# A graph network's node pass: two products of each block written in rows, their biases added on GpSimd and VectorE

## The chip, the cores and the metric

One core of a Trainium2 chip runs the program. Times are microseconds (us) of one execution on the device. The engines are named as in the profile: PE is TensorE's matmuls, PEld its weight loads, DVE VectorE, ACT ScalarE, POOL GpSimd, SP SyncE, which only issues transfers here.

## The reference, cut to what matters

Four graph layers stand one behind the other on 50,000 nodes of 128 values, 25,000 edges, each in the form `x = x + layer(relu(layernorm(x)))`. All is fp32. What a node gets with no edge, cut to its form:

```python
def own(x):                        # a node without edges
    h = relu(layernorm(x))
    for l in range(5):             # GAT: both heads' mean is h @ mean(W[l]) + bias[l]
        h = h @ W[l].mean(heads) + eb[l].mean(heads) + b[l]
        if l < 4: h = relu(h)
    x = x + h
    h = relu(layernorm(x))         # HGT: gate * ba + (1 - gate) * h
    x = x + gate * ba + (1 - gate) * h
    h = relu(layernorm(x))         # GCN
    x = x + gelu(h @ gcn_W + gcn_b)
    h = relu(layernorm(x))         # typed attention
    return x + h @ cat_W[0] + cat_b
```

The edges' part follows behind, and overwrites the rows of nodes that have some.

## The kernel before, in words

`node_pass` (L319) does the above for all nodes. The nodes are padded to 50,688 and cut into N = 132 blocks of 384 (T = 3 tiles of 128 rows, W = 384). The loop index k of every engine runs over blocks in a software pipeline written out by hand: in its iteration k, an engine does a certain step of block k, another of block k-1, and so on to k-7. Beside the blocks run 98 steps of "slots" (k < 98), two tiles each of gathered rows `xg`, which get their layer norm and scores only. Every engine's instructions go out in the order in which the code lists them; semaphores (one counter an event) tie the engines together.

What each engine does in iteration k, in order:

- **TensorE** (L581): the first product of the GAT chain for block k-1 (L603, features in partitions, 384 nodes moving, into `psZ`); its scores (L605, into `psA`); transposes of the chain's end `zT` of block k-2 back into rows (L613, into `psX`, by the helper `turn`, L584); the slots' scores (L619). Then for r = 1 to 4: product r of the chain (L627, again into `psZ`) and `to_rows` (L592), which writes h of that layer as rows with scores into `psR`. Between them: at r = 2 the transposes of `n2` (L634, into `psB`), at r = 3 those of `n3` (L640, `psC`) and the GCN product (L644, features in partitions, into `psB`), at r = 4 the last layer's product (L649, in rows, six records of 128 columns), the transposes of the next block (`psA`, L654) and slots (`psS`, L657), and the transposes of `gT`, the GELU's result, back into rows (L661, `psB`). A transpose shows as L584 in the profile.
- **ScalarE** (L664): for each r the relu with bias out of `psZ` (L681), at r = 4 the bias alone into `zT` (L684); `rows_out` (L672) of each layer; `h5c` (L704) and `hT6` (L709) at r = 2; `hT7` (L714), the normed rows of block k (L720) and slots (L728) and the GELU with bias by feature (L735) at r = 3; at the end `hT0` of block k (L738), for which the first product of the next iteration waits, and `hTs` (L742).
- **VectorE** (L471): the small operations that end in `var` (L503 to L511); the output of block k-7 (L521); `x3 = psB + x2` (L526) of block k-5; the statistics of x, of the slots and of x3 (L479); `shift` (L539, which waits for `rstd`); the normed tiles n1, n2, n3 (L493, nine); the bias `cat_b` (L558); `x1 = psX + x` (L563); `x2` (L568, which waits for ScalarE's `h5c`); two more statistics; `x1 + hgt_ba` (L573).
- **GpSimd** (L436): `rstd` by a power (L451) once `var` is there, two gathers of slot rows (L747), then three indirect transfers an iteration out of a list of 392: 196 "put" (4 bytes a row into `row_of`, L456), behind them 196 "got" (L747 into `src_row`). At k of N and more, a power of degrees (L465).
- **SyncE** (L387): loads x three blocks ahead (L391) and stores the eight tables of results (L404 to L429).

Buffers: x has six slots, `rows` two a layer, most others three. `K.by_feature[:, 0:1]` is the GCN bias with features in partitions, `K.gat_bias` that of the chain, and `K.hgt_ba` and `cat_b` are biases spread over the partitions, for rows.

Of the kernel before, what the change touches and what calls it, by code (L numbers as in the profile page):

```python
# [15 lines left out]
P = 128  # L16
# [302 lines left out]
def node_pass(nc, K, I, out):  # L319
# [10 lines left out]
    with ExitStack() as ctx:  # L330
# [15 lines left out]
        hT0, hTa, hTb, zT = (A.sb(m, [P, W]) for m in ("hT0", "hTa", "hTb", "zT"))  # L346
        hT6, gT, hT7 = (A.sb(m, [P, W]) for m in ("hT6", "gT", "hT7"))
# [7 lines left out]
            "turnedA", "hT0", "scored0", "scores0_out", "mixed", "relu", "rowed", "rows_out", "zT", "back_x",  # L355
            "turned2", "hT6", "gcn", "gelu", "back_g", "turned3", "hT7", "last",
# [28 lines left out]
        with nc.Block(no_gpsimd_drain=True) as block:  # L385
            @block.sync
            def _(eng):  # L387
# [5 lines left out]
                with nc.allow_non_contiguous_dma(reason="bias"):  # L393
                    eng.dma_start(cat_b[:, :], I.cat_b.unsqueeze(0).broadcast_to([P, D])).then_inc(s.bias_in, 16)
# [41 lines left out]
            def _(eng):  # L436
# [6 lines left out]

                steps = [("put", c) for c in range(C)] + [("got", c) for c in range(C)] 
# [3 lines left out]
                for k in range(LAST + 1):  # L448
# [5 lines left out]
                    for what, c in steps[k * per:(k + 1) * per]:  # L454
# [4 lines left out]
                        else:  # L459
                            if c == 0:  # L460
                                eng.wait_ge(s.row_put, 16 * C)
                            gather(eng, K.row_of, K.src_tm[:, c:c + 1], K.src_row[:, c:c + 1], s.row_got)
                    if k >= N:
                        c = (k - N) * 25
                        eng.tensor_tensor(K.dinv[:, c:min(c + 25, C + 2)], K.deg[:, c:min(c + 25, C + 2)],  # L465
                                          K.half[:, c:min(c + 25, C + 2)], ALU.pow).then_inc(s.dinv, 1)
# [4 lines left out]
            def _(eng):  # L471
# [26 lines left out]
                n_stats += stats_of_slots(0)  # L498
                for k in range(LAST + 1):
# [23 lines left out]
                    if is_block(b):  # L523
                        eng.wait_ge(s.back_g, b + 1)
                        eng.wait_ge(s.x2, b + 1)
                        eng.tensor_tensor(xs[:, b % SB, :, :], wide(psB), xs[:, b % SB, :, :], ALU.add).then_inc(s.x3, 1)  # L526
# [24 lines left out]
                    if is_block(b):  # L551
# [4 lines left out]
                        if b == 0:  # L556
                            eng.wait_ge(s.bias_in, 16)
# [3 lines left out]
                    if is_block(b):  # L561
                        eng.wait_ge(s.back_x, b + 1)
                        eng.tensor_tensor(x1[:, b % 2, :, :], wide(psX), x[:, b % XB, :, :], ALU.add).then_inc(s.x1, 1)  # L563
# [12 lines left out]
                    if is_block(b):  # L576
                        eng.wait_ge(s.x2, b + 1)
                        n_stats += stats_of(k + 1, at_2, xs[:, b % SB, :, :], T)

            @block.tensor  # L580
            def _(eng):  # L581
# [14 lines left out]
                for k in range(LAST + 1):  # L596
                    b = k - 1
                    if is_block(b):
                        eng.wait_ge(s.hT0, b + 1)
                        if b:  # L600
                            eng.wait_ge(s.zT, b)
# [6 lines left out]
                    if is_block(k - 2):  # L608
                        b = k - 2
                        eng.wait_ge(s.zT, b + 1)  # L610
                        if b:
                            eng.wait_ge(s.x1, b)
                        turn(psX, lambda t: zT[:, t * P:(t + 1) * P]).then_inc(s.back_x, 1)  # L613
# [8 lines left out]
                    for r in range(1, L):  # L622
                        b = k - 1
                        if is_block(b):
                            h = hTa if r % 2 else hTb
                            eng.wait_ge(s.relu, 4 * b + r)
                            eng.matmul(psZ[:, 0:W], K.gat_wm[:, r, :], h[:, :], start=True, stop=True).then_inc(s.mixed, 1)  # L627
                            to_rows(r, b, h)
                        b = k - 4
                        if r == 2 and is_block(b):  # L630
                            eng.wait_ge(s.nB2, b + 1)
                            if b:
                                eng.wait_ge(s.x3, b)
# [8 lines left out]
                        if r == 3 and is_block(b):  # L642
                            eng.wait_ge(s.hT6, b + 1)
                            eng.matmul(psB[:, 0:W], K.gcn_w[:, :], hT6[:, :], start=True, stop=True).then_inc(s.gcn, 1)  # L644
# [13 lines left out]
                        b = k - 4  # L658
                        if r == 4 and is_block(b):
                            eng.wait_ge(s.gelu, b + 1)  # L660
                            turn(psB, lambda t: gT[:, t * P:(t + 1) * P]).then_inc(s.back_g, 1)  # L661

            @block.scalar
            def _(eng):  # L664
# [9 lines left out]
                for k in range(LAST + 1):  # L674
                    b = k - 1
                    for r in range(L):
                        b = k - 1
                        if is_block(b):
                            eng.wait_ge(s.mixed, L * b + r + 1)
                            if r < L - 1:  # L680
                                eng.activation((hTb if r % 2 else hTa)[:, :], psZ[:, 0:W], ACT.Relu, bias=K.gat_bias[:, r:r + 1]  # L681
                                               ).then_inc(s.relu, 1)
                            else:
# [2422 lines left out]
```

## Time and profile before

| | |
|---|---|
| median of 3 runs | 5821.73 us (5819.69 to 5822.21) |
| the profiled execution, its own time | 5835.43 us |
| its span in the trace | 5833.6 us |
| granted TensorE clock over the span | 0.88 of full speed |
| PE busy | 4824.4 us, 83% of the span |
| DVE, ACT, POOL busy | 4143.7, 3247.3 and 3035.7 us |

The node pass is the stretch from about 138 to about 1,665 us of the span; the other two thirds are the work on edges. A share of busy time is a mean over both. In the rows below, a timeline row is: start, duration, engine, line, operation with output and inputs, number of merged instructions, and in brackets how long the engine had been idle before and who ended that. A duration of several merged instructions runs from the first's start to the last's end. A row of a stretch gives busy us and instructions (x) of PE, PEld, DVE, ACT and POOL, in this order; its DMA share is the time that packets took, as a share of 16 engines, and can pass 1 where packets queue.

### The profile page before, as it was taken

How to read it: one execution, taken by the hardware profiler on the slowest of the kernel's cores; microseconds unless marked ns; L12 is line 12 of the kernel's file. 1: busy time of each engine (PE TensorE's matmuls, PEld its weight loads, DVE VectorE, ACT ScalarE, POOL GpSimd, SP SyncE). 2: the span in 40 equal slices, each digit the busy share in tenths (PEclk: the TensorE clock that was granted, in tenths of full speed). 3: DMA queues.
4: the chain of work that ended last, by engine and by line, in shares of the span. 5: the costliest groups of instructions: out<-in, count | busy, mean ns of one | idle time of the engine just before them, and what ended most of it. 6: DMA issues, size and time to landing. Idle time of an engine off the chain costs nothing. (4 is left out here: it accounts for less than half of the span.)

```text
span 5833.6 us, 104695 instructions
## 1 busy us (share of the span) xinstructions
PE 4824.4 (83%) x29899; PEld 4142.3 (71%) x29899; DVE 4143.7 (71%) x15589; ACT 3247.3 (56%) x8537; POOL 3035.7 (52%) x2871
## 2 busy tenths in 40 slices
PE   4999999999959969969969969866995767868666
PEld 3777777777749959959969959844774656746565
DVE  4677777778867668767767768786676667847765
ACT  1777877877736636636636636543772336746500
POOL 0666666655575445445355356222651347555367
PEclk6999999999979979979979979955997778989855
DMA  2999986665545535535535435388663447845332
GB/s 69 167 216 209 210 210 209 210 203 195 192 116 128 123 77 130 117 83 127 111 89 130 104 98 134 87 244 227 151 147 79 138 132 207 233 110 114 66 92 86
DMA packets 1111146, 841.29 MB, mean 144 GB/s; under 512 B 210522, under 2 KB 1063102, under 8 KB 1110256
## 3 DMA queue, kind: packets, MB, share of 16 engines
q1 hardware_dynamic: 1030276, 706.02, 47.0%
q0 software_dynamic: 77040, 128.08, 10.5%
q8 instruction: 251, 4.11, 0.3%
q14 instruction: 315, 2.58, 0.2%
q10 hardware_dynamic: 3264, 0.50, 0.1%
HBM read 390.57 MB, written 448.11 MB: 144 GB/s over the span
## 5 line engine op out<-in xcount | busy, mean ns | idle before, releaser
L747 POOL DMA_INDIRECT gat_G<-table,k_src_row x980 | 1030.8, 1052 | 629.2 <-PE gat_psE L1523 422.5
L1520 PE MATMUL gat_psG<-gat_ends_at,gat_Gw 128*128 128x128 f32 x3920 | 718.5, 279 | 12.3 <-DVE gat_loop L1317 12.3
L1520 PEld LDWEIGHTS gat_psG<-gat_ends_at,gat_Gw 128*128 128x128 f32 x3920 | 599.9, 193 | 15.5 <-issue 12.8
L451 POOL TENSOR_TENSOR nodes_rstd<-nodes_var,k_half 128x14 f32<-128x14 f32 x138 | 360.4, 2612 | 398.1 <-DVE nodes_var L511 390.8
L1521 PE MATMUL gat_psG<-k_ident,gat_loop 128*128 128x128 f32 x1960 | 538.2, 275 | 0.0
L1446 ACT ACTIVATE gat_aggT<-gat_psG 128x512 f32<-128x512 f32 x490 | 292.5, 597 | 396.8 <-PE gat_psE L1523 396.8
L1534 PE MATMUL gat_psZ<-gat_aggT,t_gat_wh 128*128 128x256 f32 x1960 | 504.8, 380 | 1.3 <-ACT gat_hT L1453 1.3
L1523 PE MATMUL gat_psE<-gat_ends_at,gat_wex 128*128 128x128 f32 x1960 | 381.9, 277 | 0.0
L1453 ACT ACTIVATE gat_hT<-gat_psZ,t_gat_bias 128x256 f32<-128x256 f32 x490 | 232.0, 473 | 240.8 <-PE gat_psZ L1535 240.8
L1438 ACT ACTIVATE gat_loop<-gat_own,gat_al 128x128 f32<-128x128 f32 x980 | 335.0, 392 | 49.8 <-DVE gat_al L1291 49.8
L1534 PEld LDWEIGHTS gat_psZ<-gat_aggT,t_gat_wh 128*128 128x128 f32 x1960 | 335.4, 191 | 27.9 <-issue 2.1
L1312 DVE TENSOR_TENSOR gat_Gw<-gat_G,gat_al 128x512 f32<-128x512 f32 x490 | 330.6, 675 | 0.0
L1523 PEld LDWEIGHTS gat_psE<-gat_ends_at,gat_wex 128*128 128x128 f32 x1960 | 299.0, 193 | 0.0
L1535 PE MATMUL gat_psZ<-gat_aggE,t_gat_ewT 128*128 128x256 f32 x980 | 291.7, 379 | 0.0
L747 POOL DMA_INDIRECT nodes_xg<-in_x,first_dst_tm x196 | 198.6, 1013 | 175.6 <-POOLq L83 126.7
L672 ACT ACTIVATE nodes_rows<-nodes_psR 128x396 f32<-128x396 f32 x528 | 267.9, 507 | 28.6 <-PE nodes_psR L592 4.1
L1521 PEld LDWEIGHTS gat_psG<-k_ident,gat_loop 128*128 128x128 f32 x1960 | 283.0, 144 | 0.0
L592 PEld LDWEIGHTS nodes_psR<-t_ident_v,nodes_hTa 128*128 128x128 f32 x1584 | 222.1, 193 | 71.1 <-issue 2.4
L592 PEld LDWEIGHTS nodes_psR<-t_ident_v,nodes_hTb 128*128 128x128 f32 x1584 | 221.0, 192 | 70.9 <-issue 1.8
L747 POOL DMA_INDIRECT cat_edge_G<-table,k_src_row x196 | 198.6, 1013 | 133.0 <-ACT cat_edge_hm L1900 91.7
L1547 PEld LDWEIGHTS gat_psR<-t_ident_v,gat_hT 128*128 128x128 f32 x1568 | 237.1, 190 | 21.0 <-ACT gat_hT L1453 1.2
L747 POOL DMA_INDIRECT hgt_edge_G<-table,k_src_row x196 | 188.7, 963 | 110.9 <-ACT hgt_edge_hm L1900 67.9
(652 smaller groups left out, 14598.8 us busy)
## 6 DMA issues: line engine op xcount, KB each, us to landing
table<-nodes_rows SPq DMA_DIRECT2D x660, 198.0 KB
table<-nodes_n SPq DMA_DIRECT2D x396, 192.0 KB
gat_own<-table SPq DMA_DIRECT2D x490, 132.0 KB
table<-gat_rows SPq DMA_DIRECT2D x392, 132.0 KB
nodes_x<-in_x SPq DMA_DIRECT2D x132, 192.0 KB
out<-nodes_x_out SPq DMA_DIRECT2D x132, 192.0 KB
gat_ex<-in_ex_pad SPq DMA_DIRECT2D x70, 336.0 KB
gat_G<-table,k_src_row POOLq DMA_INDIRECT x980
```

Source lines behind the costliest of these rows:

```text
L451: eng.tensor_tensor(rstd[:, k % 3, :], var[:, k % 3, :], K.half[:, 0:M], ALU.pow).then_inc(s.pow, 1)
L592: mm = eng.matmul(psR[l % 2][:, t * ROWW:(t + 1) * ROWW], hT[:, t * P:(t + 1) * P], K.ident_v[:, l, :], start=True, stop=True)
L672: eng.activation(rows[:, l - 1, b % 2, :, :], wide(psR[l % 2], T, ROWW), ACT.Copy).then_inc(s.rows_out, 1)
L747: eng.indirect_dma_start(to, None, table, bass.IndirectOffsetOnAxis(ap=index, axis=0)).then_inc(sem, 16)
L1312: eng.tensor_tensor(Gw[:, i % RS, :, :, :], spread(G[:, g % RG, 2 * k:2 * k + 2, 0:D], 2, H), spread(a, 3, D), ALU.mult).then_inc(s.weighe ...
L1438: ins = eng.activation(loop[:, i % RS, t, 0, :], own[:, i % RO, t, 0:D], ACT.Copy, scale=al[:, g % 2, 1, a:a + 1])
L1446: eng.activation(aggT[:, i % RA, :, :, :].rearrange("p t h q -> p (t h q)"), psG[i % 2][:, :], ACT.Copy).then_inc(s.aggT, 1)
L1520: eng.matmul(o[:, h * P:(h + 1) * P], Gw[:, i % RS, t, h, :], ends_at[:, i % RS, t, :], start=True, stop=False)
L1521: eng.matmul(o[:, h * P:(h + 1) * P], loop[:, i % RS, t, h, :], K.ident[:, :], is_transpose=True, start=False, stop=True)
L1523: mm = eng.matmul(psE[i % 2][:, t * P:(t + 1) * P], wex[:, g % 2, c, :], ends_at[:, i % RS, t, :], start=True, stop=True)
L1534: eng.matmul(o, K.gat_wh[:, l, h, :], aggT[:, i % RA, :, h, :], start=(h == 0), stop=False)
L1535: eng.matmul(o, K.gat_ewT[:, l, :], aggE[:, i % RA, :, :].rearrange("p t q -> p (t q)"), start=False, stop=True).then_inc(s.mixed, 1)
```

## The change

The chain's last product (r = 4) and the GCN product swap their operands: the node tiles are now the stationary side, the weights move, and the result stands in rows at once (three products of 128 columns in place of one of 384 each). The transposes back into rows and ScalarE's `zT` and `gT` are gone. A bias along a row can't be ScalarE's per-partition bias, so: VectorE forms `last_b` once from the raw biases; GpSimd adds it to x ahead of time, block by block, into `xb` (six slots); VectorE adds `gcn_b` to the GCN product into `z6`, at the end of its iteration; ScalarE's GELU reads `z6` and writes `g6`, now as the last operation of its iteration; and L526 adds `g6`, out of SBUF, in the next one. Four small loads of biases stand ahead of the first loads of x.

```diff
+        z6, g6 = A.sb("z6", [P, T, D]), A.sb("g6", [P, T, D])
+        xb = A.sb("xb", [P, XB, T, D])
...
+                    for h in range(GAT_HEADS):
+                        eng.dma_start(bias_raw[:, h, :], I.gat_eb[L - 1:L, h * D:(h + 1) * D].broadcast_to([P, D])).then_inc(s.raw_bias, 16)
+                    eng.dma_start(bias_raw[:, 2, :], I.gat_b[L - 1:L, :].broadcast_to([P, D])).then_inc(s.raw_bias, 16)
+                    eng.dma_start(gcn_b[:, :], I.gcn_b.unsqueeze(0).broadcast_to([P, D])).then_inc(s.bias_in, 16)
...
                 for b in range(3):
...
+                def with_bias(b):
+                    if b == 0:
+                        eng.wait_ge(s.bias, 2)
+                    eng.wait_ge(x_in[b % XB], 16 * (b // XB + 1))
+                    if b >= XB:
+                        eng.wait_ge(s.x1, b - XB + 1)
+                    eng.tensor_tensor(xb[:, b % XB, :, :], x[:, b % XB, :, :], spread(last_b[:, :], 1, T), ALU.add).then_inc(s.xb, 1)
+
...
+                    if is_block(k):
+                        with_bias(k)
                     if k >= N:
...
                 n_stats += stats_of_slots(0)
+                eng.wait_ge(s.raw_bias, 48)
+                eng.tensor_tensor(last_b[:, :], bias_raw[:, 0, :], bias_raw[:, 1, :], ALU.add).then_inc(s.bias, 1)
+                eng.wait_ge(s.bias, 1)
+                eng.scalar_tensor_tensor(last_b[:, :], last_b[:, :], 1.0 / GAT_HEADS, bias_raw[:, 2, :], ALU.mult, ALU.add).then_inc(s.bias, 1)
...
                     b = k - 5
                     if is_block(b):
-                        eng.wait_ge(s.back_g, b + 1)
+                        eng.wait_ge(s.gelu, b + 1)
...
-                        eng.tensor_tensor(xs[:, b % SB, :, :], wide(psB), xs[:, b % SB, :, :], ALU.add).then_inc(s.x3, 1)
+                        eng.tensor_tensor(xs[:, b % SB, :, :], g6[:, :, :], xs[:, b % SB, :, :], ALU.add).then_inc(s.x3, 1)
...
-                            eng.wait_ge(s.bias_in, 16)
+                            eng.wait_ge(s.bias_in, 32)
...
                     b = k - 2
                     if is_block(b):
-                        eng.wait_ge(s.back_x, b + 1)
-                        eng.tensor_tensor(x1[:, b % 2, :, :], wide(psX), x[:, b % XB, :, :], ALU.add).then_inc(s.x1, 1)
+                        eng.wait_ge(s.mixed4, b + 1)
+                        eng.wait_ge(s.xb, b + 1)
+                        eng.tensor_tensor(x1[:, b % 2, :, :], wide(psX), xb[:, b % XB, :, :], ALU.add).then_inc(s.x1, 1)
...
                     if is_block(b):
...
+                    b = k - 4
+                    if is_block(b):
+                        if b == 0:
+                            eng.wait_ge(s.bias_in, 32)
+                        eng.wait_ge(s.gcn, b + 1)
+                        if b:
+                            eng.wait_ge(s.gelu, b)
+                        eng.tensor_tensor(z6[:, :, :], wide(psB), spread(gcn_b[:, :], 1, T), ALU.add).then_inc(s.z6, 1)
...
                         if b:
-                            eng.wait_ge(s.zT, b)
...
                         eng.matmul(psZ[:, 0:W], K.gat_wm[:, 0, :], hT0[:, :], start=True, stop=True).then_inc(s.mixed, 1)
...
-                    if is_block(k - 2):
-                        b = k - 2
-                        eng.wait_ge(s.zT, b + 1)
-                        if b:
-                            eng.wait_ge(s.x1, b)
-                        turn(psX, lambda t: zT[:, t * P:(t + 1) * P]).then_inc(s.back_x, 1)
...
                         if is_block(b):
...
-                            eng.matmul(psZ[:, 0:W], K.gat_wm[:, r, :], h[:, :], start=True, stop=True).then_inc(s.mixed, 1)
+                            if r < L - 1:
+                                eng.matmul(psZ[:, 0:W], K.gat_wm[:, r, :], h[:, :], start=True, stop=True).then_inc(s.mixed, 1)
+                            else:
+                                if b:
+                                    eng.wait_ge(s.x1, b)
+                                for t in range(T):
+                                    mm = eng.matmul(psX[:, t * D:(t + 1) * D], h[:, t * P:(t + 1) * P], K.gat_wm[:, r, :],
+                                                    start=True, stop=True)
+                                mm.then_inc(s.mixed4, 1)
                             to_rows(r, b, h)
...
                             if b:
-                                eng.wait_ge(s.x3, b)
+                                eng.wait_ge(s.z6, b)
                             turn(psB, lambda t: n2[:, b % RB, t, :]).then_inc(s.turned2, 1)
...
                         if r == 3 and is_block(b):
...
-                            eng.matmul(psB[:, 0:W], K.gcn_w[:, :], hT6[:, :], start=True, stop=True).then_inc(s.gcn, 1)
+                            for t in range(T):
+                                mm = eng.matmul(psB[:, t * D:(t + 1) * D], hT6[:, t * P:(t + 1) * P], K.gcn_w[:, :], start=True, stop=True)
+                            mm.then_inc(s.gcn, 1)
                         if r == 4 and is_block(b):
...
-                        b = k - 4
-                        if r == 4 and is_block(b):
-                            eng.wait_ge(s.gelu, b + 1)
-                            turn(psB, lambda t: gT[:, t * P:(t + 1) * P]).then_inc(s.back_g, 1)
...
                         b = k - 1
                         if is_block(b):
-                            eng.wait_ge(s.mixed, L * b + r + 1)
                             if r < L - 1:
+                                eng.wait_ge(s.mixed, (L - 1) * b + r + 1)
...
-                            else:
-                                eng.activation(zT[:, :], psZ[:, 0:W], ACT.Identity, bias=K.gat_bias[:, r:r + 1]).then_inc(s.zT, 1)
...
                             if is_block(b):
...
-                            b = k - 4
-                            if is_block(b):
-                                eng.wait_ge(s.gcn, b + 1)
-                                eng.activation(gT[:, :], psB[:, 0:W], ACT.Gelu, bias=K.by_feature[:, 0:1]).then_inc(s.gelu, 1)
...
+                    b = k - 4
+                    if is_block(b):
+                        eng.wait_ge(s.z6, b + 1)
+                        if b:
+                            eng.wait_ge(s.x3, b)
+                        eng.activation(g6[:, :, :], z6[:, :, :], ACT.Gelu).then_inc(s.gelu, 1)
```

## Rows read from the trace of the kernel before

**Rows 1.** Busy times by stretch: start:end, its us, engines, clock, DMA share, GB/s

```profile
300.00:500.00 200.00, 187.52 (x1198) 149.89 (x1196) 155.25 (x626) 158.40 (x398) 133.81 (x105) 1.00 1.05 211
500.00:600.00 100.00, 94.46 (x601) 75.56 (x601) 77.06 (x312) 79.80 (x201) 65.81 (x53) 1.00 0.98 211
900.00:1270.00 370.00, 347.83 (x2215) 277.91 (x2213) 287.11 (x1151) 293.94 (x739) 238.00 (x189) 1.00 0.64 209
1280.00:1620.00 340.00, 330.23 (x2074) 263.75 (x2073) 283.50 (x1113) 259.16 (x593) 178.49 (x128) 1.00 0.57 193
```

**Rows 2.** Timeline, one iteration with slots: the ring of ScalarE and TensorE

```profile
809.31 0.91 PE L603 MATMUL nodes_psZ<-nodes_hT,first_gat_wm 128*128 128x384 f32 x2 [0.69 <-ACT nodes_hT L738]
...
813.88 0.58 ACT L681 ACTIVATE nodes_hTa<-nodes_psZ,t_gat_bias 128x384 f32<-128x384 f32 x1 [0.41 <-PE nodes_psZ L627]
...
818.97 0.58 ACT L735 ACTIVATE nodes_gT<-nodes_psB,k_by_feature 128x384 f32<-128x384 f32 x1
818.97 0.49 PE L584 MATMUL nodes_psA<-k_ident,nodes_rows 128*128 128x128 f32 x3
...
819.89 0.52 ACT L672 ACTIVATE nodes_rows<-nodes_psR 128x396 f32<-128x396 f32 x1
...
820.27 0.52 ACT L738 ACTIVATE nodes_hT<-nodes_psA 128x384 f32<-128x384 f32 x1
820.64 0.42 ACT L742 ACTIVATE nodes_hTs<-nodes_psS 128x256 f32<-128x256 f32 x1
...
820.85 0.91 PE L603 MATMUL nodes_psZ<-nodes_hT,first_gat_wm 128*128 128x384 f32 x2 [0.69 <-ACT nodes_hT L738]
```

**Rows 3.** Timeline, VectorE in these iterations

```profile
815.59 0.56 DVE L568 TENSOR_TENSOR nodes_xs<-nodes_xs,nodes_h5c 128x384 f32<-128x384 f32 x1 [1.39 <-ACT nodes_h5c L704]
...
820.19 0.56 DVE L526 TENSOR_TENSOR nodes_xs<-nodes_psB,nodes_xs 128x384 f32<-128x384 f32 x1 [0.46 <-PE nodes_psB L584]
...
822.29 0.85 DVE L493 TENSOR_SCALAR nodes_n<-nodes_x,nodes_negmean,nodes_rstd 128x128 f32<-128x128 f32 x3
```

**Rows 4.** Timeline, GpSimd: one iteration from power to power

```profile
807.04 2.61 POOL L451 TENSOR_TENSOR nodes_rstd<-nodes_var,k_half 128x14 f32<-128x14 f32 x1 [2.48 <-DVE nodes_var L511]
...
815.25 0.98 POOL L456 DMA_INDIRECT row_of<-first_slot_row_tm,k_node_tm  x1 [0.30 <-issue]
...
818.57 2.62 POOL L451 TENSOR_TENSOR nodes_rstd<-nodes_var,k_half 128x14 f32<-128x14 f32 x1 [2.35 <-DVE nodes_var L511]
```

**Rows 5.** DMA issues from 300 to 400 us: KB each, median us to landing

```profile
resid<-nodes_xg SPq DMA_DIRECT2D x9, 128.0 KB, 10.6
```

**Rows 6.** Timeline, the same iterations: TensorE's transposes and the products beside them

```profile
810.65 0.52 PE L584 MATMUL nodes_psX<-k_ident,nodes_zT 128*128 128x128 f32 x3
811.01 0.51 PE L619 MATMUL nodes_psS<-t_gat_v,nodes_hTs 128*128 128x4 f32 x4
...
814.25 0.36 PEld L584 LDWEIGHTS nodes_psB<-k_ident,nodes_n 128*128 128x128 f32 x3
...
818.30 0.83 PE L649 MATMUL nodes_psC<-k_cat_out,nodes_hT 128*128 128x128 f32 x6
```

**Rows 7.** GpSimd's elementwise operations: ns min/median/max, first and last start us

```profile
L843 POOL TENSOR_SCALAR_AFFINE_SELECT tiles_after<-tiles_ones x2: 349/349/349, 3.3 to 3.6; 128x196 f32<-128x196 f32 x2
...
L2253 POOL TENSOR_TENSOR hgt_sums_rstd<-hgt_sums_power,k_dinv x98: 189/195/197, 4457.6 to 4754.2; 128x2 f32<-128x2 f32 x98
...
L2249 POOL TENSOR_TENSOR hgt_sums_power<-hgt_sums_var,k_half x98: 695/801/822, 4456.7 to 4753.4; 128x2 f32<-128x2 f32 x98
```

**Rows 8.** Timeline, an iteration without slots

```profile
1394.04 0.49 PE L584 MATMUL nodes_psA<-k_ident,nodes_rows 128*128 128x128 f32 x3
...
1394.57 0.53 ACT L738 ACTIVATE nodes_hT<-nodes_psA 128x384 f32<-128x384 f32 x1
...
1396.10 0.58 ACT L681 ACTIVATE nodes_hTa<-nodes_psZ,t_gat_bias 128x384 f32<-128x384 f32 x1 [1.00 <-PE nodes_psZ L603]
...
1396.74 0.30 PEld L627 LDWEIGHTS nodes_psZ<-nodes_hTa,first_gat_wm 128*128 128x128 f32 x2
```

More of the change, by code:

```diff
@@ L345, in node_pass @@
         shift = A.sb("shift", [P, 3, M])
-        hT0, hTa, hTb, zT = (A.sb(m, [P, W]) for m in ("hT0", "hTa", "hTb", "zT"))
-        hT6, gT, hT7 = (A.sb(m, [P, W]) for m in ("hT6", "gT", "hT7"))
+        hT0, hTa, hTb = (A.sb(m, [P, W]) for m in ("hT0", "hTa", "hTb"))
+        hT6, hT7 = (A.sb(m, [P, W]) for m in ("hT6", "hT7"))
+        z6, g6 = A.sb("z6", [P, T, D]), A.sb("g6", [P, T, D])
+        xb = A.sb("xb", [P, XB, T, D])
+        last_b, gcn_b = A.sb("last_b", [P, D]), A.sb("gcn_b", [P, D])
+        bias_raw = A.sb("bias_raw", [P, 3, D])
         hTs = A.sb("hTs", [P, SC * P])
@@ L354, in node_pass @@
             "nA", "nB1", "nB2", "nC", "nS", "h5c", "x1", "x1b", "x2", "x3", "x3b", "finished",
-            "turnedA", "hT0", "scored0", "scores0_out", "mixed", "relu", "rowed", "rows_out", "zT", "back_x",
-            "turned2", "hT6", "gcn", "gelu", "back_g", "turned3", "hT7", "last",
+            "turnedA", "hT0", "scored0", "scores0_out", "mixed", "relu", "rowed", "rows_out", "mixed4",
+            "turned2", "hT6", "gcn", "z6", "gelu", "turned3", "hT7", "last", "raw_bias", "bias", "xb",
             "turnedS", "hTs", "scoredS", "scoresS_out", "dinv", "row_put", "row_got"))
```

## The prediction

> **What bounds the kernel now.** I read the busy times by stretch first. TensorE is busy 94% of the stretch with slots (300 to 1,270 us) and 97% behind it, at the full clock [rows 1]. That looks like a TensorE bound, but a busy share says nothing of what an iteration waits for. So the timeline of one iteration comes next. From one start of L603 to the next are 11.54 us [rows 2], and these split exactly: 4.57 us on TensorE's side until ScalarE starts its third relu (809.31 to 813.88), 6.91 us in which ScalarE works without a gap until `hT0` is written (813.88 to 820.27 + 0.52), and 0.06 us to the start of L603, which waited for `hT0` for 0.69 us [rows 2]. The ring is TensorE, ScalarE, TensorE. VectorE waits 1.39 us inside it at L568 and 0.46 us at L526 [rows 3]; GpSimd waits 2.35 us for `var` [rows 4]. Third, the transfers: from 300 to 500 us the DMA share is 1.05, then 0.98, and 0.64 once the 4-byte "puts" are over (33 iterations from 900 to 1,270), at the same GB/s and the same iteration [rows 1]; a store issued between 300 and 400 us lands after 10.6 us [rows 5]. The queue is full there, though nobody waits for it yet.
>
> **The change, part by part** (per iteration unless said).
>
> *TensorE, first part of the ring.* The `psX` transposes go. L619 started 0.36 us behind them (810.65 to 811.01) [rows 6] and the second product waits only for its place: -0.36.
>
> *ScalarE's part.* GELU and `zT` go out of the gapless run: from the GELU's start to that of the next L672 are 0.92 us [rows 2]. But `hT0` also needs the `psA` transposes, which end at 818.97 + 0.49 = 819.46 [rows 2]; so it can start at 819.50, not 820.27: -0.77. TensorE is late next.
>
> *The `psB` transposes back into rows* stand behind those of `psA`, where TensorE waited for `hT0` anyway: 0.
>
> *The two swapped products.* Each becomes six records of 128 columns, the form of L649, whose six take 0.67 us up to the next group's start (818.30 to 818.97) [rows 2, 6]. I put +0.05 for both together. Lower end 0; upper end, if four more weight loads each stayed uncovered at 0.12 us (three take 0.36 [rows 6]), +1.0. L649 shows them covered, so I stay low.
>
> *VectorE.* `z6` is one more 128x384 operation out of PSUM, 0.56 us like L526 [rows 3], before `var`. L526 itself only changes its source: 0. What moves is its releaser. The GELU is now behind `hTs`, which starts 0.21 us before L603 (820.64 against 820.85) and takes 0.42 [rows 2]; so the GELU (0.58, as now) ends some 0.75 us behind L603, and L526 starts at +0.8, where it stood at -0.66 [rows 2, 3]: 1.45 us later. The 1.39 us wait at L568 [rows 3] swallows that but for 0.06. The tighter place is `n2`: from L526's start to the first normed tile are 2.10 us, and six tiles take about 1.6 at the pace of [rows 3], so `n2` is there at +4.5; TensorE wants it at 814.25 [rows 6] less 809.31 and 0.36, at +4.58. It just fits. Behind `n2` wait the `psB` transposes, `hT6` and the rest of the ring, so I add 0.04.
>
> *GpSimd.* Power, two gathers and three puts run from 807.04 to 815.25 + 0.98 = 816.23, 9.19 us [rows 4]. Behind them comes `xb`. The trace has no such add. Low end: an operation with one input took 0.349 us for 196 elements, a product of two inputs 0.195 us for 2 [rows 7], so 0.8 ns an element and 0.50 us for 384. High end: the power goes from 0.70 us (2 elements) to 2.61 (14) [rows 4, 7], 0.16 us an element, 61 us for 384; but on equal shapes the product took 0.195 against 0.80, so an add is near the low end. Two or three streams at 0.8 ns an element give 0.8 to 1.1; I take 1.0, and 0.1 for its start. GpSimd is then busy 10.3 us.
> From its figure for a 2,048-element add, the Trainium skill (GPSIMD Engine Reference, "Performance versus the Vector engine") gives, as an estimate, about 1.0 us as well, by which the sum stays.
>
> *Beyond GpSimd:* `xb` of block k is read two iterations later, which hides its latency. Four bias loads and two small VectorE operations stand before the first iteration: +2 once; each load is short beside an iteration.
>
> So the compute allows 11.54 - 0.36 - 0.77 + 0.05 + 0.04 = 10.5 us: -1.04 an iteration, in the stretch with slots.
>
> *Transfers.* The same bytes in less time. With 1.05 as "full", an iteration can't go below 11.54 x share / 1.05: 11.54 from 300 to 500 us (I allow -0.2, since the share was falling already), 10.77 from 500 to 600, then under 10.5 [rows 1]. Ends: no gain there, and the full gain if the queue just grows longer.
>
> *Iterations without slots* (33 of 10.3 us, by 593 ScalarE instructions at 18 each in 340 us [rows 1]). Here `hT0` starts at 1394.57, right behind the `psA` transposes (1394.04 + 0.49), and the second product's weights at 1396.74, right behind the relu (1396.10 + 0.58) [rows 8]. Neither removal is on the path: 0, and +0.05 each for the swap.
>
> *Sum:* up to 300 us 0; 17 iterations x 0.2 = 3.5; 9 x 0.77 = 6.7; (1,270 - 600) / 11.54 = 58 x 1.04 = 60.4; less 1.6 and 2: **-67 us**. The profiled execution took 5835.4 us, so 5768; it stood 13.7 us above the median of 5821.7, hence **5755**.
>
> **The rivals.**
>
> *Transfers decide (0.17).* The whole stretch with puts stays full, up to 900 us; only 32 iterations x 1.04 gain: -33, less 3.6: 5792. For: landing of 10.6 us [rows 5]. Against: 0.98 falling further.
>
> *Transfers never decide (0.13).* Nobody waits for the stores now, and the buffers take a longer queue: 84 iterations x 1.04 = 87, some 5 more before 300 us, less 3.6: 5733.
>
> *GpSimd becomes the bound (0.12).* An add of 1.5 us makes 9.19 + 0.1 + 1.5 = 10.8: 58 x 0.74 = 43, with the 10 from before 600 us, less 3.6: 5772. For: nothing shows an add of this size. Against: the slope of [rows 7].
>
> *GpSimd's add blocks VectorE (0.06).* A two-element power took 0.695 us at best and 0.801 in the median [rows 7]; waiting for a port beside VectorE's work would be one reason for such 0.1 us, but the rows don't say it.
> The Trainium skill (SBUF — State Buffer, "Who interferes with whom") speaks against the change here: two-input VectorE operations and GpSimd's reads lock each other out for a whole instruction.
> As a mechanism of this kernel: the add lies where VectorE does `z6` and the five small ones up to `var`. Held up, `var` comes up to 1.0 us late, the power with it: 9.19 + 1.1 + 0.75 = 11.0, so 58 x 0.5, with 8 from before 600 us, less 3.6: 5788.
> By that rule the forecast would lose half its gain; the trace shows at most that 0.1 us of it.
>
> *Slower (0.06).* The same place, dearer: once the add with its waits passes 11.54 - 9.19 - 0.1 = 2.25 us, GpSimd's turn is longer than today's iteration. At 3.0 us: 12.3, +0.75 x 97 iterations, + 3.6: 5898. For and against as for the bound above.
>
> *No change (0.06).* `n2` comes 1 us late, since the GELU at the end waits for `z6` or gathers land late: VectorE is the ring, 11.5, in all: 5822. Against: 0.46 and 1.39 us of waits that it has to give [rows 3].
>
> **How the numbers follow.** Forecast 0.40, with rivals 0.17, 0.13, 0.12, 0.06, 0.06, 0.06. The likeliest gives 5755. The range runs from beyond the "never decide" case, 5715, to past the contention case, 5800; outside lie slower, no change and some tails. A difference under 0.2%, 11.6 us, can't be told from none: faster 0.86, same 0.08, slower 0.06.
>
> **What would show it.** Right: L451 starts every 10.4 to 10.6 us behind 600 us, and every 10.3 to 10.4 without slots; no `psX` or second `psB` group of L584; ScalarE's L738 starts right behind the `psA` transposes; the add takes about 1.0 us; GpSimd's wait for `var` shrinks from 2.35 to 0.2; L526 waits for the GELU, L568 hardly waits. Wrong: GpSimd without idle time, small VectorE operations of more than 0.2 us, stores that ScalarE's L672 waits for, or a ring below 10.4.

## The result, and the profile after

| | before | after |
|---|---|---|
| median of 4 runs each, side by side | 5821.97 us (5819.69 to 5824.38) | 5782.01 us (5774.21 to 5789.50) |
| the profiled execution, its own time | 5835.43 us | 5780.01 us |
| its span; granted TensorE clock | 5833.6 us; 0.88 | 5778.3 us; 0.88 |
| node pass, first to last instruction | 131.1 to 1668.8 us | 131.9 to 1619.7 us |

The ratio is 0.9931, 95% interval 0.9914 to 0.9948: 40 us faster, inside the range of 5715 to 5800 us, where 67 were forecast. In the profiles the node pass gives 49 us, up to the start of the last power, and the stages on edges, which are unchanged, another 6. The starts of the power (L451 before, L467 after), k = 0 to 137, show where, beside the forecast for about the same stretch:

| iterations | before, us each (median) | after | difference of the stretch | forecast |
|---|---|---|---|---|
| start, k = 0 | | | +2.2 | +2 |
| 0 to 13 | | | -10.7 | 0 |
| 13 to 66, slots and puts | 11.54 | 10.96 | -26.9 | -37 |
| 66 to 98, slots and gots | 11.54 | 10.51 | -30.8 | -33 |
| 98 to 133, no slots | 10.33 | 10.82 | **+14.5** | +1.6 |
| 133 to 137 | | | +2.6 | |

(The forecast's -67 by its own terms: -3.5 - 6.7 - 27 up to 900 us, -33 from 900 to 1,270, +1.6 and +2.) The gain of 1.03 us an iteration is there, but only in the third line. With puts more than a quarter is missing (some 3 us of it at one place: the first "got" waits 4.35 us for the last "put", 1.40 before), and without slots the kernel is slower than before.

The busy times by stretch of the kernel after (columns as in [rows 1]):

```profile
300.00:500.00 200.00, 188.69 (x1294) 158.07 (x1293) 192.99 (x678) 163.21 (x403) 162.74 (x128) 1.00 0.97 222
500.00:600.00 100.00, 94.50 (x648) 79.02 (x646) 96.86 (x339) 81.34 (x201) 81.40 (x64) 1.00 0.91 222
...
1250.00:1600.00 350.00, 309.19 (x2024) 254.10 (x2024) 323.57 (x1125) 244.03 (x526) 219.47 (x151) 0.98 0.52 179
```

Against [rows 1], VectorE went from 155 to 193 us in the first 200, 78% to 96%. The work of before in the shorter iteration (0.78 x 11.54 = 9.0 us) and one more operation of 0.54 make 87% of 10.96 us; some 1.1 us an iteration are neither. The DMA share fell (1.05 to 0.97) although the same bytes go in less time (211 to 222 GB/s): the transfers are not what holds it, and the iteration takes 10.96 us at a share of 0.97 as at 0.91. Nor does the clock: the 0.98 of the last row comes from a fall behind 1,580 us, at the pass's end; the iterations of 10.82 us ran at 1.00. The groups of instructions name VectorE's surplus. Columns: line, engine, operation, output and inputs, shapes, count, then busy us and mean ns of one, then the idle time before. The first two rows are of 300 to 600 us, the next two of 900 to 1,200, the last two of 1,250 to 1,600:

```profile
L525 DVE TENSOR_TENSOR nodes_diff<-nodes_st 128x14 f32<-128x14 f32 x28 | 44.1, 1574 | 0.0
L458 POOL TENSOR_TENSOR nodes_xb<-nodes_x,nodes_last_b 128x384 f32<-128x384 f32 x28 | 28.5, 1017 | 0.3
...
L591 DVE TENSOR_TENSOR nodes_xs<-nodes_xs,nodes_h5c 128x384 f32<-128x384 f32 x29 | 17.2, 594 | 0.0
L525 DVE TENSOR_TENSOR nodes_diff<-nodes_st 128x14 f32<-128x14 f32 x28 | 11.8, 421 | 0.0
...
L591 DVE TENSOR_TENSOR nodes_xs<-nodes_xs,nodes_h5c 128x384 f32<-128x384 f32 x33 | 55.9, 1693 | 0.5 <-ACT nodes_h5c L732 0.5
L525 DVE TENSOR_TENSOR nodes_diff<-nodes_st 128x14 f32<-128x14 f32 x33 | 5.6, 168 | 0.0
```

A subtraction of 14 elements takes 1,574 ns with puts, and 168 without slots. L591, which was 0.56 us as L568 [rows 3], takes 1,693 ns without slots. Neither changed its shape. Which of the two is long depends on which meets GpSimd's new add, L458. A VectorE instruction that takes longer than its work needs because of that add is called held from here on. The timeline with puts (after) shows the meeting:

```profile
801.07 0.83 PE L677 MATMUL nodes_psB<-k_gcn_w,nodes_hT 128*128 128x128 f32 x6
...
801.74 0.83 PE L657 MATMUL nodes_psX<-first_gat_wm,nodes_hTb 128*128 128x128 f32 x6
...
803.35 1.59 DVE L525 TENSOR_TENSOR nodes_diff<-nodes_st 128x14 f32<-128x14 f32 x1
...
803.75 0.49 PE L615 MATMUL nodes_psA<-k_ident,nodes_rows 128*128 128x128 f32 x3
803.88 1.01 POOL L458 TENSOR_TENSOR nodes_xb<-nodes_x,nodes_last_b 128x384 f32<-128x384 f32 x1
...
804.28 0.49 ACT L762 ACTIVATE nodes_hT<-nodes_psA 128x384 f32<-128x384 f32 x1 [0.17 <-PE nodes_psA L615]
...
804.83 0.91 PE L633 MATMUL nodes_psZ<-nodes_hT,first_gat_wm 128*128 128x384 f32 x2 [0.36 <-ACT nodes_hT L762]
...
804.93 0.53 ACT L772 ACTIVATE nodes_g<-nodes_z 128x384 f32<-128x384 f32 x1
...
805.24 0.17 DVE L533 SCALAR_TENSOR_TENSOR nodes_var<-nodes_square,nodes_spread 128x14 f32<-128x14 f32 x1
...
805.49 2.61 POOL L467 TENSOR_TENSOR nodes_rstd<-nodes_var,k_half 128x14 f32<-128x14 f32 x1 [0.61 <-DVE nodes_var L533]
...
805.82 0.55 DVE L548 TENSOR_TENSOR nodes_xs<-nodes_g,nodes_xs 128x384 f32<-128x384 f32 x1
...
808.21 0.17 DVE L561 TENSOR_TENSOR nodes_shift<-nodes_negmean,nodes_rstd 128x14 f32<-128x14 f32 x1 [0.28 <-POOL nodes_rstd L467]
...
814.84 1.01 POOL L458 TENSOR_TENSOR nodes_xb<-nodes_x,nodes_last_b 128x384 f32<-128x384 f32 x1
...
815.76 0.91 PE L633 MATMUL nodes_psZ<-nodes_hT,first_gat_wm 128*128 128x384 f32 x2 [0.36 <-ACT nodes_hT L762]
...
816.47 2.61 POOL L467 TENSOR_TENSOR nodes_rstd<-nodes_var,k_half 128x14 f32<-128x14 f32 x1 [0.61 <-DVE nodes_var L533]
```

`hT0` (L762) starts right behind the `psA` transposes, as forecast: the old ring is broken. The new one runs through GpSimd's turn and the held `diff`: add ends 804.89, `diff` 0.05 behind it at 804.94, `var` at 805.41, power 805.49 to 808.10, two gathers, three puts, add again; 816.47 - 805.49 = 10.98 us. VectorE also waits 0.28 us for `rstd`. Without slots:

```profile
1402.74 0.55 DVE L586 TENSOR_TENSOR nodes_x<-nodes_psX,nodes_xb 128x384 f32<-128x384 f32 x1
...
1403.20 1.90 DVE L591 TENSOR_TENSOR nodes_xs<-nodes_xs,nodes_h5c 128x384 f32<-128x384 f32 x1
...
1403.66 1.02 POOL L458 TENSOR_TENSOR nodes_xb<-nodes_x,nodes_last_b 128x384 f32<-128x384 f32 x1
...
1406.66 0.53 DVE L609 TENSOR_TENSOR nodes_z<-nodes_psB,nodes_gcn_b 128x384 f32<-128x384 f32 x1
...
1407.23 0.52 ACT L772 ACTIVATE nodes_g<-nodes_z 128x384 f32<-128x384 f32 x1
...
1407.85 2.61 POOL L467 TENSOR_TENSOR nodes_rstd<-nodes_var,k_half 128x14 f32<-128x14 f32 x1 [3.17 <-DVE nodes_var L533]
...
1410.57 0.17 DVE L561 TENSOR_TENSOR nodes_shift<-nodes_negmean,nodes_rstd 128x14 f32<-128x14 f32 x1 [0.68 <-POOL nodes_rstd L467]
```

Here GpSimd has a wait of 3.17 us for `var` and is no bound; but L591 is held: 1.90 us in place of 0.55, so for 1.35 us, and all behind it on VectorE is late: `z6`, `var`, the power, `shift`, `n2`.

### The profile page after: what moved, and what is told of

It reads as the page before. It is cut to its first block and busy times, and to the rows that moved or that the text cites. A ratio compares the mean times of both kernels' runs of the same rounds, so it can differ in the third digit from the quotient of the medians.

```text
span 5778.3 us, 105883 instructions
## 1 busy us (share of the span) xinstructions
PE 4762.5 (82%) x30163; PEld 4142.2 (72%) x30163; DVE 4316.8 (75%) x15723; ACT 3219.1 (56%) x8405; POOL 3188.7 (55%) x3003
## 3 DMA queue, kind: packets, MB, share of 16 engines
q0 software_dynamic: 77040, 128.08, 10.3%
## 5 line engine op out<-in xcount | busy, mean ns | idle before, releaser
L467 POOL TENSOR_TENSOR nodes_rstd<-nodes_var,k_half 128x14 f32<-128x14 f32 x138 | 360.5, 2612 | 187.7 <-DVE nodes_var L533 187.7
L472 POOL DMA_INDIRECT row_of<-first_slot_row_tm,k_node_tm x196 | 212.6, 1085 | 59.8 <-issue 59.8
```

The source lines that it names most:

```text
L467: eng.tensor_tensor(rstd[:, k % 3, :], var[:, k % 3, :], K.half[:, 0:M], ALU.pow).then_inc(s.pow, 1)
```

## The experiments

Three theories were set against each other. **A**: GpSimd's add holds the instructions of VectorE that read two SBUF tiles. **B**: the new order of operations is bound by itself, whatever GpSimd does. **C**: the transfers are the bound. All ratios are to the kernel before on the same chip. That kernel took 5830 us on the chip of the second series, but 6174, 6135 and 6172 us on those of the first, third and last. On the latter the iterations with slots are irregular in every kernel profiled there (11.4 to 13.1 us in the median) and I found no cause; the iterations without slots take 10.3 us on all where nothing is held, so readings from those chips rest on that stretch and on the ratios. The kernel before was not profiled on them.

**No add on GpSimd** (first series; the last layer's bias is left out).

```diff
-                    if is_block(k):
-                        with_bias(k)
...
-  eng.tensor_tensor(x1[:, b % 2, :, :], wide(psX), xb[:, b % XB, :, :], ALU.add)
+  eng.tensor_tensor(x1[:, b % 2, :, :], wide(psX), x[:, b % XB, :, :], ALU.add)
```

> GpSimd's add of last_b is left out, and L586 adds x itself, so the last layer's bias of the chain is missing in x1; everything else is the changed kernel. Theory A (GpSimd's add and VectorE's two-input SBUF operations lock each other out; with puts the turn add, var, power, five transfers, add is the ring of 10.96 us, without slots the add holds L591): the iteration falls to 10.4 to 10.5 us in the whole stretch with slots, 300 to 850 us too, and to 10.3 without slots; L525 takes 0.17 and L591 0.55 us everywhere; median 5730 to 5745. Theory B (the new order alone sets the time: z6 on VectorE and the GELU at ScalarE's end make VectorE's part the ring): 10.96, 10.51 and 10.82 us stay within 0.1, median 5775 to 5785. Theory C (transfers set the stretch with puts): 10.9 stays there, and only the rest gets faster, median 5755 to 5765.

Ratio 0.9874 (0.9857 to 0.9890), nearest to A's median (0.984 to 0.987 as a ratio). Iteration without slots 10.32 us, `diff` 0.17 throughout. With slots it took 11.57 us, not A's 10.4 to 10.5, and more than the 10.9 that C named.

**The add behind the power**, once `shift` is written.

```diff
+                    if is_block(k):
+                        eng.wait_ge(s.shift, k + 1)
+                        with_bias(k)
                     if is_slots(k + 2):
                         gather_slots(k + 2)
...
-                    if is_block(k):
-                        with_bias(k)
```

> The same work as the changed kernel; GpSimd's add moves from the end of its iteration to just behind the power, and waits for VectorE's shift, so that it runs beside the nine normed tiles, which read one SBUF tensor each. Theory A, if normed tiles aren't held: L525 back to 0.17 us, L591 to 0.55, GpSimd's turn 9.2 + 1.1 plus its wait for var under 10.6; iterations 10.5 with slots, 10.3 to 10.4 without; median 5735 to 5750. If the normed tiles are held as well: they take 1 us longer, n2 comes late, 11.2 us or more: median 5800 and above. Theory B: no difference from the changed kernel, 5775 to 5785.

Ratio 0.9966 (0.9953 to 0.9978). `diff` is at 0.17 us and the add of `h5c` free; a new victim shows in the timeline without slots:

```profile
1505.78 1.54 DVE L512 TENSOR_SCALAR nodes_n<-nodes_x,nodes_negmean,nodes_rstd 128x128 f32<-128x128 f32 x3
1505.95 1.03 POOL L458 TENSOR_TENSOR nodes_xb<-nodes_x,nodes_last_b 128x384 f32<-128x384 f32 x1 [0.60 <-DVE nodes_shift L562]
...
1507.24 1.62 DVE L512 TENSOR_SCALAR nodes_n<-nodes_xs,nodes_negmean,nodes_rstd 128x128 f32<-128x128 f32 x6
```

Three normed tiles take 1.54 us where they took 0.85 [rows 3]. They read one tile each, so what the add holds is wider than "two inputs". The iteration without slots is 10.41 us, so little of this reaches it there; with slots it is 13.1 us, against 11.57 with no add on the same chip. The expectation's second branch (normed tiles held, ratio of 0.996 and above) is the one that came.

**The chain's half alone** (the GCN product, its GELU and its transposes as before; add kept) and **the GCN half alone** (chain as before, no add), cut to the products; waits and the moved additions are left out:

```diff
 chain alone:  -  matmul(psB[:, t * D:(t + 1) * D], hT6[:, t * P:(t + 1) * P], K.gcn_w[:, :])   x3
               +  matmul(psB[:, 0:W], K.gcn_w[:, :], hT6[:, :])
               +  activation(gT[:, :], psB[:, 0:W], ACT.Gelu, bias=K.by_feature[:, 0:1])
               +  turn(psB, lambda t: gT[:, t * P:(t + 1) * P])
 GCN alone:    the same four lines the other way round, in the kernel before
```

> Only the chain's half of the change: the GCN product, the GELU out of PSUM and the transposes back are as before; the last product is in rows and GpSimd adds last_b at the end of its iteration. Theory A: with puts GpSimd's turn holds it at about 10.9 to 11.0 as in the changed kernel, behind the puts 10.7 (11.54 less 0.36 and 0.46), without slots 10.3 to 10.8 by what the add meets; median 5765 to 5785. Theory B: without z6 and the moved GELU there is nothing to lose, 10.7 in the whole stretch with slots, 10.3 without: median 5750 to 5757.

> Only the GCN's half: z6 on VectorE, the GELU last on ScalarE, no transposes of its result; the chain's end is as before (zT, psX transposes) and GpSimd adds nothing. Theory A: ScalarE's part loses one operation, 11.54 less 0.46 = 11.1 in the whole stretch with slots, 10.3 without; L525 and L591's counterparts stay at 0.18 and 0.56 us; median 5780 to 5790. Theory B: the moved GELU is late for n2, so 11.3 or more with slots and over 10.5 without: median 5805 to 5830.

Ratios 0.9913 (0.9899 to 0.9926) and 0.9987 (0.9978 to 0.9996). With slots each takes 12.9 us, where both halves without the add take 11.57; A had 10.9 and 11.1, B 10.7 and at least 11.3. The GCN half's ratio is the one that B named (5805 to 5830 us, 0.997 and above): alone it gives 0.13%, a miss for A. The chain's half gives 0.87% even with the add in it, the two without the add 1.26%. Why the GCN half is worth so little alone stays open, since the kernel before was not profiled on this chip. Without slots both take 10.3 us, the chain's half with GpSimd's add in it: the add's own time costs nothing there. The timeline there:

```profile
1503.65 1.01 POOL L458 TENSOR_TENSOR nodes_xb<-nodes_x,nodes_last_b 128x384 f32<-128x384 f32 x1
...
1504.61 0.56 DVE L591 TENSOR_TENSOR nodes_xs<-nodes_xs,nodes_h5c 128x384 f32<-128x384 f32 x1 [0.81 <-ACT nodes_h5c L726]
```

The add falls into VectorE's wait for `h5c`, and meets nothing. In the kernel after that wait is gone, since `h5c` comes earlier against L591, and the add meets L591 itself.

**Before and after again, the bias on TensorE, and two adds** (second series, one chip).

> The kernel before, profiled beside the other kernels of this series, so that they are compared on one chip. All theories: iterations of 11.5 to 13 us with slots and 10.33 without, and no held instruction on VectorE: diff 0.17 us, the add of h5c 0.56 us throughout.

> The changed kernel, profiled beside the others. Theory A (GpSimd's add holds VectorE): without slots 10.8 us for an iteration, 0.5 above the kernel before on the same chip, and there the add of h5c at 1.9 us where it is 0.56 in the kernel before; its ratio to the kernel before lies above that of the two kernels of this series that have no such add. Theory B (the new order alone) and C (transfers): 10.8 too, but then the kernel with the bias on TensorE has it as well.

Ratios 0.9992 (0.9983 to 1.0001) and 0.9946 (0.9931 to 0.9960). The first is the same kernel twice, and shows what the ratios can tell apart. 11.54 and 10.33 us before, 10.96 and 10.82 after, as in the first pair. Only the stretch of gots differs: 10.78 us, and `diff` at a mean of 1,471 ns where the first profile has 10.51 and 421. The same kernel holds `diff` there for 1.3 us in one execution and for 0.25 us in another, where it starts behind the add's start, and 0.27 us an iteration hangs on it.

```diff
 bias on TensorE: (no add on GpSimd, x1 = psX + x)
+  eng.matmul(psX[:, 0:W], K.ones[0:1, :], spread(last_b[0:1, :], 1, T), start=True, stop=False)
   eng.wait_ge(s.relu, 4 * b + r)
...
-                                                    start=True, stop=True)
+                                                    start=False, stop=t == T - 1)
 two adds:
+  eng.tensor_tensor(spare[:, b % XB, :, :], x[:, b % XB, :, :], spread(last_b[:, :], 1, T), ALU.add)
```

> The last layer's bias is put into psX by a product of one row of ones with the bias (one matmul of K = 1 and 384 columns ahead of the wait for ReLU 4), so that GpSimd has no elementwise add and VectorE adds x itself, as before the change. It computes all that the changed kernel does. Theory A: 10.3 to 10.4 us for an iteration without slots (the changed kernel 10.8), diff and the add of h5c unheld, ratio to the kernel before 0.987 to 0.990, 0.4 to 0.6 per cent below the changed kernel. Theory B: 10.8 without slots, ratio as the changed kernel. Theory C: 10.3 without slots, but with slots no gain over the changed kernel.

Ratio **1.0062** (1.0048 to 1.0075): slower than before, and a miss for theory A's number. Nothing is held (`diff` 171 ns), yet 11.61 us with puts and 11.36 without slots. The timeline of TensorE:

```profile
802.60 0.83 PE L678 MATMUL nodes_psB<-k_gcn_w,nodes_hT 128*128 128x128 f32 x6
...
803.36 0.91 PE L652 MATMUL nodes_psX<-nodes_last_b,k_ones 1*128 1x384 f32 x2
...
804.20 0.94 PE L658 MATMUL nodes_psX<-first_gat_wm,nodes_hTb 128*128 128x128 f32 x6
...
806.31 0.49 PE L612 MATMUL nodes_psA<-k_ident,nodes_rows 128*128 128x128 f32 x3
```

From the GCN product to the chain's are 1.60 us, where the kernel after has 0.67 (801.07 to 801.74): one row of ones costs as much as a full product of 384 columns. The 0.93 us lie ahead of the `psA` transposes, so on the ring: 10.32 + 0.93 = 11.25 of the 11.36 measured without slots. Read the other way, 11.61 - 0.93 = 10.68 is an estimate of the ring with puts when nothing is held; a high one, since the kernel after had 10.51 with gots. TensorE had no slack to give.

> GpSimd adds twice, the second time into a spare tile that nobody reads. Theory A: what VectorE has two SBUF inputs for is held twice as often or as long: held instructions beside both adds, GpSimd's round with puts rises by the second add (1.0 us and some 0.5 of waiting), the iteration without slots by 0.5 to 1.5 us, to 11.3 to 12.3; with puts, where GpSimd is the ring, by 1.0 to 1.5; ratio to the kernel before above 1.0. Theory B: GpSimd waits for var 0.61 us with puts and several us without slots, so the second add costs up to 0.4 us with puts and nothing without slots (10.8).

Ratio 1.0138 (1.0122 to 1.0153). Iterations 11.91 us with puts (10.96 with one add) and 11.77 without slots (10.82): +0.95 in both, for which A had 1.0 to 1.5 with puts and B at most 0.4. Groups from 300 to 600 us, then from 1,280 to 1,550:

```profile
L526 DVE TENSOR_TENSOR nodes_diff<-nodes_st 128x14 f32<-128x14 f32 x26 | 64.8, 2493 | 0.0
L459 POOL TENSOR_TENSOR nodes_spare<-nodes_x,nodes_last_b 128x384 f32<-128x384 f32 x26 | 26.3, 1010 | 0.0
...
L592 DVE TENSOR_TENSOR nodes_xs<-nodes_xs,nodes_h5c 128x384 f32<-128x384 f32 x23 | 65.5, 2849 | 0.0
L468 POOL TENSOR_TENSOR nodes_rstd<-nodes_var,k_half 128x14 f32<-128x14 f32 x23 | 60.1, 2614 | 72.8 <-DVE nodes_var L534 72.8
```

`diff` goes from 1.57 to 2.49 us, L592 (L591 of after, 1.90 us in the mean of the second series) to 2.85. The same instruction is held through both adds, for 1.0 us more. Without slots GpSimd waited 72.8 / 23 = 3.2 us an iteration for `var`, so its own time can't be the reason: nobody waits for the second add's result, and by theory B it costs nothing there. This is the run that decides for A without slots; the chain's half alone, with one add that meets nothing and 10.3 us, is its counterpart.

**The add on VectorE, no add again, and a copy in place of the add** (third series), and the first of these once more.

```diff
 on VectorE, behind var:
+  eng.tensor_tensor(xb[:, k % XB, :, :], x[:, k % XB, :, :], spread(last_b[:, :], 1, T), ALU.add).then_inc(s.xb, 1)
 copy:
-  eng.tensor_tensor(xb[:, b % XB, :, :], x[:, b % XB, :, :], spread(last_b[:, :], 1, T), ALU.add).then_inc(s.xb, 1)
+  eng.tensor_copy(xb[:, b % XB, :, :], x[:, b % XB, :, :]).then_inc(s.xb, 1)
```

> GpSimd's add x + last_b goes to VectorE, right behind var, where in the kernel with the bias on TensorE it waits 1.32 us for psC; it computes all that the changed kernel does. Theory A (what the changed kernel loses, it loses by GpSimd's add holding VectorE and by its time in GpSimd's round): the 0.54 us of the add lie in VectorE's wait, nothing is held, iterations of 10.3 to 10.5 us without slots (10.8 in the changed kernel) and 10.4 to 10.7 with puts (10.96), ratio to the kernel before 0.987 to 0.990, the changed kernel 0.993 to 0.995. Theory B (the new order is bound elsewhere): VectorE's own 0.54 us or TensorE set the ring, 10.8 or more in both stretches, ratio 0.994 or above.

> The changed kernel without the add; the last layer's bias is left out of the result. It was run once on a chip on which all kernels took some 6 per cent more. Theory A: without slots 10.32, with slots 10.4 to 10.6, nothing held, ratio 0.985 to 0.989, within 0.1 per cent of the kernel with the add on VectorE. Theory B: 10.8 without slots. Theory C (transfers bound the stretch at 300 to 600 us): 10.32 without slots, but 10.9 or more with puts, although GpSimd then has 9.2 us of work in a round.

> GpSimd copies x instead of adding the bias to it: an instruction with one SBUF input in the place of one with two; the last layer's bias is left out of the result. Theory A in its wide form (any elementwise instruction of GpSimd holds VectorE's instructions with two SBUF inputs): diff and the add of h5c held as in the changed kernel, for as long as the copy lasts and 0.3 to 0.4 us more; iteration without slots 10.5 to 10.8. Theory A in its narrow form (two inputs on both sides are needed): nothing held, 10.3 without slots, ratio within 0.2 per cent of the kernel without the add.

> The kernel with the add on VectorE once more, since its first series ran on a chip on which all kernels took some 5 per cent more. If this series runs on a chip on which the kernel before takes some 5825 us: Theory A: 10.3 to 10.4 us for an iteration without slots and 10.4 to 10.7 with puts, against 10.82 and 10.96 in the changed kernel; ratio to the kernel before 0.985 to 0.989, some 5745 us, 40 us below the changed kernel. Theory B: 10.8 in both stretches and the changed kernel's ratio, 0.993 to 0.995. On the slower chip: 0.986 again.

On VectorE: 0.9860 (0.9843 to 0.9876) and 0.9881 (0.9863 to 0.9899), 10.33 us without slots in both; B had 10.8. No add: 0.9859 (0.9843 to 0.9876), 10.33. So the add costs VectorE nothing without slots, and nothing in the whole time that the intervals, 10 us to either side, can tell. With slots the profiled executions took 11.76 to 11.9 us, and 11.5 with no add and with the copy, not the 10.4 to 10.7 that A named; that number is not confirmed anywhere. It is also not below the 10.9 that C named, so with slots, on these chips, C stays open. The kernel after was not run on these chips, and the one with the add on VectorE not on the chip of the second series. That it beats the kernel after rests on ratios to the kernel before on different chips (0.986 and 0.988 against 0.993 and 0.995), and on 10.3 against 10.8 us without slots. The timeline there, of the first of them:

```profile
1408.30 0.55 DVE L538 TENSOR_TENSOR nodes_xb<-nodes_x,nodes_last_b 128x384 f32<-128x384 f32 x1
1408.46 2.86 POOL L467 TENSOR_TENSOR nodes_rstd<-nodes_var,k_half 128x14 f32<-128x14 f32 x1 [3.71 <-DVE nodes_var L532]
...
1408.79 0.56 DVE L546 TENSOR_TENSOR nodes_x_out<-nodes_psC,nodes_xs 128x384 f32<-128x384 f32 x1
...
1410.05 0.56 DVE L551 TENSOR_TENSOR nodes_xs<-nodes_g,nodes_xs 128x384 f32<-128x384 f32 x1 [0.70 <-ACT nodes_g L775]
```

The add lies in what was a wait, and now it is GpSimd that gives way: its power takes 2.86 us in place of 2.61. The copy: 0.9843 (0.9830 to 0.9856). GpSimd's copy takes 0.62 us in the median, and where it meets an instruction of VectorE without slots it holds it as well, but briefly (the bias is left out of this kernel's result):

```profile
1403.98 0.92 DVE L580 TENSOR_TENSOR nodes_xs<-nodes_xs,nodes_cat_b 128x384 f32<-128x384 f32 x1
...
1404.59 0.66 POOL L458 COPY nodes_xb<-nodes_x 128x384 f32<-128x384 f32 x1
```

0.92 us against 0.56, and 10.36 us an iteration. The narrow form of A (two inputs on both sides) is refuted, the wide one holds, though its 10.5 to 10.8 us were too much.

## Why the prediction was right, and where it was off

- **The ring's new length: right.** 10.5 us was the sum, 10.51 the median with gots, where `diff` is held for only 0.25 us. `hT0` starts behind the `psA` transposes, GELU and `zT` are off the path, L591 hardly waits (L568: 1.39 us). `n2` has no margin, as feared: TensorE waits 0.22 us for it at 809.98.
- **The swapped products: right.** L657 and L677 are six records each, and the next group starts 0.67 and 0.67 us behind (801.07, 801.74, 802.41), against 0.67 for L649 [rows 2, 6].
- **GpSimd's add: right in size, wrong in effect.** 1.01 us where 1.0 stood. The step that failed is the term "GpSimd is then busy 10.3 us", which priced the add in GpSimd's time alone and put VectorE's delay at nothing; it was 1.42 us at `diff` and 1.35 us at L591. The rival "GpSimd's add blocks VectorE", with 0.06, was the one that held. It named the ring (9.19 + 1.1 + 0.75 = 11.0) and with puts the trace shows 10.96. The rule of the Trainium skill (SBUF — State Buffer, "Who interferes with whom") agrees with the trace here: `diff` ends 0.05 us behind the add. I gave it little because [rows 7] showed only 0.1 us, but those rows are powers of two elements, and not even the power of 14 elements holds VectorE (L548 above), so they said nothing of an add. The estimate of 1.0 us from the Trainium skill's figure (GPSIMD Engine Reference, "Performance versus the Vector engine", 4,497 ns for 2,048 elements) was worked out too high: by elements it is 0.84 us, and the trace has 1.01.
- **The rival's reach: too small and too large.** It forecast 11.0 in all 58 iterations behind 600 us; the 32 with gots ran at 10.5. It had nothing for the iterations without slots, where the loss is largest: some 0.49 us each, +14.5 in all.
- **Transfers: wrong.** I gave the stretch up to 500 us 3.5 us, and up to 300 us none. The share fell to 0.97 while the rate rose to 222 GB/s, and 13 iterations up to k = 13 already gained 10.7 us. The iterations with puts ran at 10.96 us from the start, where 11.34 stood up to 500 us, and at the same 10.96 when the share had fallen to 0.91: on this chip theory C is out as their bound. The transfers were to take about 18 us of the gain; in their place the add took about 24 (53 iterations of 0.46) and the late "got" 3. That these two errors largely cancel there (-27 against -37) is luck.
- **From profile to median: 15 us.** The profiled execution of before stood 13.7 us above its median and I carried that over; that of after stands 2.0 us below. 67 - 40 = 27: 18 from the node pass, 15 from this, less the 6 that the other stages gave.
- **The range: held by its margin.** 5782 us lies nearer to the contention rival (5788, chance 0.06) than to the forecast (5755). It is inside because the range was drawn past that rival.

## What to carry to other kernels

Before moving an elementwise operation to an idle GpSimd, ask which of VectorE's instructions lies beside it, and price the move with that instruction's delay: here 1.0 us of "free" work held VectorE for 1.35 to 1.42 us, and what it cost depended on who was met. Look for a wait of the busy engine first: VectorE took the same add in 0.55 us, in a wait, and the iteration without slots stayed at 10.33 us. And a share of busy time below 100% is no slack: TensorE was busy 94 to 97% [rows 1], and 0.93 us more of it went into the iteration nearly in full (10.32 to 11.36).

## What the runs showed of the hardware

- A held instruction of VectorE waits from its own start until GpSimd's add has ended: `diff` ends 0.05 us behind it, L591, which needs 0.55, ends 0.42 behind it. The start of `diff` lies 0.53 us ahead of the add's recorded one (803.35 and 803.88), although 0.17 us was all it needed. So either the lock begins before the record does, or the record is late.
- The power, which also reads two tiles, doesn't hold VectorE over its 2.61 us: L548, with two SBUF inputs, runs in 0.55 us inside it. "For a whole instruction", as the rule of the Trainium skill cited above has it, fits the add and not the power. The power takes 0.25 us more (2.86) where VectorE's add had started 0.16 us before it.
- GpSimd's copy of 128x384 took 0.49 to 0.81 us, 0.62 in the median, its add with two inputs 1.01. Beside the copy, L580 was held for 0.36 us, and ended at 1404.90, 0.35 us before the copy's recorded end (1405.25): the copy does not hold for as long as its record lasts, as the add does.
- A product with one row (K = 1, 384 columns, fp32) took 0.91 us, as one with 128 rows, and pushed its successor back by 0.93.
